# A row maximum split in two, statistics behind routing work, and dispatch sends one step sooner, in a vision-text attention and mixture-of-experts kernel

## What is computed

```python
h = tok_ref(x, ...)                      # patches -> 36 tokens, with a layer norm
h = concatenate([h, txt], axis=1)        # (64, 113, 128)
h = h + attn_ref(layernorm(h), Wq, Wkv, Wo, bo)
h = h + ffn_ref(layernorm(h), gate_w, expert_bias, shared..., expert...)

# attn_ref: 8 heads of 64
scores = einsum('bqhd,bkhd->bhqk', q * scale, k).astype(bfloat16)
probs  = softmax(scores, axis=-1)        # row maximum subtracted first
out    = einsum('bhqk,bkhd->bqhd', probs, v) @ Wo + bo
# ffn_ref: a shared expert, and 3 of 16 experts per token
affinity = sigmoid(xf @ gate_w.T)
_, sel = top_k(affinity + expert_bias, 3)
gating = affinity[sel] / sum(affinity[sel])
out = shared(xf) + sum(gating * expert[sel](xf))
```

## Time and profile before

| | |
|---|---|
| median of 3 runs | 810.36 us (809.16 to 811.22) |
| the profiled execution | 811.83 us, its span 810.0 us |
| busy in the span | PE 631.4 us (78%), DVE 586.3 (72%), ACT 437.6 (54%), POOL 553.6 (68%) |
| sends, L610 | 192 on POOL, 200.2 us busy, 1043 ns each |
| expert rows out, L629 | 186 on POOL, 182.0 us busy, 979 ns each |
| row maximum, L1324 | 64 on DVE, 69.7 us busy, 1089 ns each |
| chain that ended last | DVE 25%, PE 22%, issue 13%, POOL 10%, DMA 8%, ACT 6% |

### The profile page before, as it was taken

One profiled execution on the slowest core, in us unless ns is written; L12 is line 12 of the kernel. 1 busy time (PEld: TensorE's weight loads), 2 busy tenths in 40 slices (PEclk: granted clock), 3 DMA queues, 4 the chain that ended last, 5 costly groups with the idle time before them and its releaser, 6 DMA issues.

```text
span 810.0 us, 20105 instructions
## 1 busy us (share of the span) xinstructions
PE 631.4 (78%) x6122; PEld 532.1 (66%) x6122; DVE 586.3 (72%) x2030; ACT 437.6 (54%) x1044; POOL 553.6 (68%) x696
## 2 busy tenths in 40 slices
PE   6667899999999999999999679663999889872000
PEld 4445778888888888888888557542888677762000
DVE  0687899999999999999999937343566565653244
ACT  2546878888888888888887623211343233220000
POOL 4364122687878878787877877777577777777464
PEclk9977999999999999999999959967999999997555
DMA  9910000011111111011111245535666565881697
GB/s 315 262 34 19 1 3 1 25 34 33 33 34 33 33 34 33 30 33 36 31 34 33 85 123 149 150 118 164 200 200 197 182 194 175 247 270 35 172 337 223
DMA packets 66444, 88.02 MB, mean 109 GB/s; under 512 B 11612, under 2 KB 58848, under 8 KB 66186
## 3 DMA queue, kind: packets, MB, share of 16 engines
q1 hardware_dynamic: 30420, 34.76, 15.4%
q10 hardware_dynamic: 23824, 28.68, 12.1%
q0 software_dynamic: 12096, 23.30, 8.5%
HBM read 57.32 MB, written 30.87 MB: 109 GB/s over the span
## 4 chain that ended last, share of the span: by engine, by line
DVE 25%; PE 22%; issue 13%; POOL 10%; DMA 8%; ACT 6%; SPq 2%; ACTq 1%; DVEq 0%; POOLq 0%
POOL expert_rows L629 6%; DMA x2t<-expert_rows 4%; DMA expert_rows<-yb,dst_i 3%; PE bank L893 3%; DVE mx L1324 3%; PE bank L687 3%; PE bank L783 2%; POOL dispatched L610 2%; DVE s L1329 2%; DVE vr L1368 2%; PE bank L797 2%; PE bank L902 2%; ACT p L1020 2%; DVE st L1341 2%; DVE o L1362 1%
## 5 line engine op out<-in xcount | busy, mean ns | idle before, releaser
L610 POOL DMA_INDIRECT dispatched<-pay,sloti x192 | 200.2, 1043 | 53.5 <-issue 52.5
L629 POOL DMA_INDIRECT expert_rows<-yb,dst_i x186 | 182.0, 979 | 61.3 <-issue 48.9
L1054 ACT ACTIVATE xe<-bank 128x256 f32<-128x256 f32 x93 | 35.7, 384 | 156.6 <-PE bank L882 132.0
L687 PE MATMUL bank<-xt,wqkv 128*128 128x452 f32 x384 | 100.3, 391 | 7.1 <-issue 5.9
L1445 DVE TENSOR_TENSOR hide<-bank,sge 128x256 f32<-128x256 f32 x93 | 39.3, 422 | 69.4 <-ACT sge L1059 35.3
L687 PEld LDWEIGHTS bank<-xt,wqkv 128*128 128x128 f32 x384 | 67.9, 193 | 14.0 <-issue 8.0
L1324 DVE TENSOR_REDUCE mx<-s 113x8 bf16<-113x904 bf16 x64 | 69.7, 1089 | 2.1 <-ACT s L1026 1.7
L836 PE MATMUL bank<-kt,qt 64*113 64x113 f32 x1024 | 67.1, 270 | 5.1 <-DVE h L1339 5.1
L1455 DVE TENSOR_TENSOR yb<-bank,gd 128x256 f32<-128x256 f32 x93 | 38.9, 418 | 43.4 <-DMA expert_rows<-yb,dst_i 39.9
L893 PE MATMUL bank<-xe,kt 128*128 128x256 f32 (+1 forms) x296 | 66.8, 355 | 2.6 <-issue 2.4
L1026 ACT ACTIVATE s<-bank 113x452 bf16<-113x452 f32 x128 | 63.1, 550 | 5.9 <-PE bank L836 5.8
(11 more groups left out here) (209 smaller groups left out, 1743.3 us busy)
## 6 DMA issues: line engine op xcount, KB each, us to landing
kt<-in_w_ffn ACTq DMA_DIRECT2D x74, 192.0 KB
xs_all<-dispatched SPq DMA_DIRECT2D x77, 140.0 KB
x2t<-expert_rows SPq DMA_DIRECT2D x16, 672.0 KB
vr<-in_w_ffn ACTq DMA_DIRECT2D x35, 192.0 KB
out_h<-h ACTq DMA_DIRECT2D x16, 224.0 KB
x2t<-in_x ACTq DMA_DIRECT2D x4, 864.0 KB, 9.8
x2t<-in_x SPq DMA_DIRECT2D x4, 864.0 KB, 11.3
dispatched<-pay,sloti POOLq DMA_INDIRECT x192
```

The lines of the kernel that those rows point to most:

```text
L610: pool.indirect_dma_start(out=xs_dram[:, :], out_offset=bass.IndirectOffsetOnAxis(ap=sloti[:, q % (PAYS // GRP), b, c:c + 1], axis=0), in_ ...
L629: pool.indirect_dma_start(out=y_dram[:, :], out_offset=bass.IndirectOffsetOnAxis(ap=dst_i[:, slot, j:j + 1], axis=0), in_=yb[t % RW][:, j, ...
L687: m = nc.tensor.matmul(dst, wqkv[:, a, at:at + 128], xg[:, b, :], start=(j == 0), stop=(j == 2))
```

## The change

The row maximum becomes two operations: an elementwise maximum of the first 57 and the last 57 of the 113 scores of each row (the middle one is in both), in bf16 into a new tile `mh`, and a reduction over 57. The first one stands ahead of the second norm (L1319), the second one behind it. The routing operation of point 1 moves from behind L1346 to ahead of L1341. `SENDS` begins one step sooner, and in a step that places a group all sends of the step are issued at its end: 3 sends in each of the steps 10 to 57, 4 in each of 58 to 64, 8 in step 65.

```diff
-SENDS = [3 * max(0, min(n - 10, 48)) + 4 * max(0, min(n - 58, 6)) for n in range(B + 1)] + [B * TOPK - 12]
+SENDS = [3 * max(0, min(n - 9, 48)) + 4 * max(0, min(n - 57, 7)) for n in range(B + 1)] + [B * TOPK - 12]
...
+        mh = sb("mh", [128, H, TP // 2], BF16)
...
-                cuts = [begin, min(begin + 1, end), min(begin + 2, end), end]
+                cuts = [begin, begin, begin, end] if n in PLACED else [begin, min(begin + 1, end), min(begin + 2, end), end]
...
+                if ok(n):
+
+                    after(dve, "s_copied", n)
+                    nc.vector.tensor_tensor(mh[0:T, :, :], s16[i][0:T, :, 0:TP // 2], s16[i][0:T, :, T - TP // 2:T],
+                                            ALU.max).then_inc(S["half_max"], 1)
                 if ok(n - 3):
                     after(dve, "rs2_done", n - 3)
...
-                    after(dve, "s_copied", n)
-                    nc.vector.reduce_max(mx[i][0:T, :], s16[i][0:T, :, 0:T], AX.X).then_inc(S["max_done"], 1)
+                    after(dve, "half_max", n)
+                    nc.vector.reduce_max(mx[i][0:T, :], mh[0:T, :, :], AX.X).then_inc(S["max_done"], 1)
...
                     nc.vector.tensor_tensor(row(n - 2), bank[3][0:T, 0:D], row(n - 2), ALU.add).then_inc(S["h_done"], 1)
+                routing(o, k, 1)
+                if ok(n - 2):
+
                     after_all(dve, ("txt_in", 32), ("h_done", n - 2, 1))
                     nc.vector.bn_stats(st2[0:T, i, :], row(n - 2)).then_inc(S["st2_raw"], 1)
...
                                             ALU.subtract).then_inc(S["xl_copied"], 1)
-                routing(o, k, 1)
                 if ok(n - 2):
```

More of the change, by code:

```diff
@@ L257, in build @@
             "st1_raw st1_done mean1_done ve1_done rs1_done xn_ready xt_done xt_copied qa_done qb_done q_copied k_copied "
-            "v_done v1_done vr_done v_ready "
+            "v_done v1_done vr_done v_ready half_max "
             "s_done s_copied max_done mx2_done sub_done exp_done pt_done pt_copied av_done rec_done o_ready ot_done ot_copied "
```

## The result

The changed kernel took 800.72 us (796.57 to 802.19, 4 runs) against 810.79 us (809.16 to 812.5, 4 runs) for the kernel before: a ratio of 0.9863, 95% interval [0.9826, 0.9901]. All ratios here are those on record, from the fast runs alone, and need not equal the quotient of the two medians. The forecast was 797.0, range 792 to 804. So it is faster, by about 10 us rather than 13. The profiled execution lasted 800.95 us (span 799.1, granted clock 0.901) against 811.83 (span 810.0).

What follows compares the result with a forecast made beforehand. VectorE and TensorE were taken to bound the steps together, GpSimd from about step 59. Rounds 8.2 us plus sends 5.1 us gave 13.3 off the profiled 811.83, 798.5; as a median 797.0, range 792 to 804.

Steps and rivals of the forecast that it cites:

- rival 1: VectorE's elementwise maximum runs at full price because of odd-length rows; a round gains 0.40 us, 800 us in all; chance 0.12.
- The term for 4q+8: Moving the routing operation in step 4q+8 shortens L1339 to L1352 from 1.22 to 1.04 us, a gain of 0.18.
- Rival 2: The moved routing operation covers none of VectorE's wait; a round gains 0.20 us, 803 us in all; chance 0.09.
- Loop B: Path over VectorE, two TensorE steps and one VectorE-bound step: 24.63 us a round, falling to 24.06 as the new bound.
- TensorE's own floor is 4 x 5.68 + 0.28 = 23.0: Least time TensorE needs for a round of four steps, 23.0 us, below the forecast round of 24.06.
- 13 x 0.63 = 8.2: Steps 7 to 58 are 13 rounds, each gaining 0.63 us: 8.2 us in all.
- 8 instead of 12: 4 x 1.28 = 5.1 us: GpSimd in step 65 has four fewer sends at 1.28 us each, so all after it comes 5.1 us sooner.
- rival 3: Tiles don't start sooner because TensorE or the loads hold them; only 8.2 us gained, 802 us; chance 0.09.
- now wait for L1238 ... 0.1 to 0.2 us late costs nothing: In placing steps GpSimd's sends wait for L1238; 0.1 to 0.2 us late costs nothing while GpSimd waits about 1 us.
- The lighter steps before gain nothing that I count: The steps before step 7 were counted with no gain.
- Rival 4: GpSimd's sends hold VectorE's elementwise maximum to 1.0 us rather than 0.31; 13 us slower, 823 us; chance 0.06.
- Rival 5: Nothing moves: the round stays at 24.7 us and the sends' gain goes into later waits, 810 us; chance 0.04.

Runs made afterwards that it cites:

- Experiment 6: Changed kernel with `mh` in fp32, so the elementwise maximum is not all bf16, on the slow chip: 916.53 us, ratio 0.997 to the kernel before.
- experiment 1: Kernel before with only the new `SENDS` and `cuts`: 805.97 us beside 811.75 for the kernel before, ratio 0.9903.
- experiment 2: Changed kernel with `SENDS` and `cuts` of before, both VectorE edits kept: 804.13 us, ratio 0.9896 to the kernel before.
- experiment 3: Changed kernel with the routing operation back in its old place, split maximum and early sends kept: 805.55 us, ratio 0.9913 to the kernel before.
- experiment 4: Changed kernel with the row maximum in one operation again, moved operation and early sends kept: 799.25 us, ratio 0.9846 to the kernel before.
- experiment 12: Changed kernel with early statistics spread over steps 1 to 4 and the maximum directly ahead of the reduction: 793.79 us, ratio 0.9807 to the kernel before.
- experiment 5: Changed kernel again, unaltered, as a control on the next, slow chip: 914.1 us beside 918.09 for the kernel before, ratio 0.9992.
- experiment 8: Changed kernel with one of a placing step's three early sends put off to the next step, slow chip: 909.57 us, ratio 0.9907 to the kernel before.
- experiment 7: Changed kernel with the first-norm statistics of two early groups spread over steps 1 to 4, slow chip: 908.17 us, ratio 0.9897 to the kernel before.
- experiment 9: Changed kernel with the early statistics spread over steps 1 to 4, on a third chip: 793.96 us beside 809.56 for the kernel before, ratio 0.9798.
- experiment 10: Changed kernel with early statistics spread over steps 1 to 4 and the one-operation row maximum: 797.08 us, ratio 0.9847 to the kernel before.
- experiment 11: Changed kernel with early statistics spread over steps 1 to 4 and one early send per placing step put off: 795.73 us, ratio 0.983 to the kernel before.

## Why the prediction was right, and where it was not

**The split.** The maximum was to last 0.39 us with a successor at 0.31, the reduction 0.62: measured 0.401, 0.31 and 0.621. Experiment 6 shows that rival 1's condition (full price) did not hold and what it would cost. The wait without its cover costs 0.12 where I said 0.17. The gain of 0.145 us a step of VectorE's time is there (0.31 and 0.54 for 1.00); that all of it would shorten the round was the wrong part, see below.

**The move.** `h` to the aggregate was forecast at 0.86 (4q+7) and 1.04 (4q+8) and measured at 0.77 and 0.85, so the gains were 0.34 and 0.37 rather than 0.25 and 0.18. In 4q+7, L1345 to L1350 takes 0.39 with L1179 between them; in the step at 276.68 it takes 0.38 with nothing between them: the moved operation is free. The term for 4q+8 was mis-sized: "0.19 (L1339) + 0.46 + 0.39" charged the moved operation with 0.46, and in its new place it takes 0.27 (270.60 to 270.87). The means of its group, 499 ns where it stood and 346 ns where it stands, say that this is no single case. In its old place it started 0.49 us behind the start of a send of GpSimd (298.35 and 297.86), in the new one it starts 0.07 us ahead of one. It has two operands in SBUF, so I take the send for the cause. In its old place it took 0.53 us or more in 11 of 16 cases, and in all 11 it ended within 0.03 us of a send's end, as if that had released it. But the other five ran at 0.34 to 0.36 us, and three of them also started during a send or a row out (322.99 behind a send at 322.15, 444.99 and 490.52); in the changed kernel all 16 ran at 0.34 to 0.36, three of them so placed. So that is argued, not shown.

Rival 2 falls by experiments 1 to 4: moving this one operation takes 0.53 us off a round without the split, and 0.44 with it. The sentence that rival 2 quotes from the Trainium skill (VectorE: DVE Perf Modes, section The DRAIN you can't avoid) does not carry over to these instructions. The trace disagrees: 0.38 us from `h` to its statistics against 0.28 of duration, and 0.43 against 0.31 in experiment 12.

**The round.** I forecast 24.06 from Loop B. It came to 23.75, and Loop B was not the bound. The step that failed is "TensorE's own floor is 4 x 5.68 + 0.28 = 23.0". I had taken the floor from one step and added the ranks. In the changed kernel TensorE is busy 23.41 us in a round and idle 0.34 before L688, by "issue" and not by a wait for any engine: 23.75 together, 0.75 above my floor. The number alone does not show this, since Loop B with the gains that were measured would be 24.63 - 0.34 - 0.37 - 0.145 = 23.78. What shows it is that TensorE's wait for `o`, through which Loop B runs, is gone, and that the split is worth 0.08 a round behind the move where Loop B has it at 0.145. The earlier trace rows had TensorE at 23.68 of 24.68 us. With the 0.42 us of issue in the same timeline that reads as a floor of 24.1, which is 0.35 too high: as the rounds get shorter, TensorE's busy time shrinks too, from 23.65 to 23.39 in the mean of 12 rounds, for the same matmuls. So that sum would not have given 23.75 either, but it would have shown how near the floor was.

A second part is the base: I took one round of 24.69, while the rounds of before average 24.47. The base was 0.22 too high and the forecast round 0.31 too high, so that the gain, 0.63 forecast and 0.72 measured, came out nearly right. That 13 x 0.63 = 8.2 met the measured 8.7 is in part luck. Of the 0.72, 0.11 to 0.16 comes with the sends, which I had put at nothing; by what path I can't show.

**The sends at the end.** "8 instead of 12: 4 x 1.28 = 5.1 us" measured 5.2, and experiments 1 and 2 (11.8 and 16.9 us) show that it is the sends alone. "5.1 us reach the end" held: from the first to the last row out it is 256.8 us after 257.5. So rival 3 is out, on a chip without the idle stretches of experiment 5.

**The sends in steps 58 and 64.** Here a step of the prediction failed: the placing step's sends "now wait for L1238 ... 0.1 to 0.2 us late costs nothing". The wait costs more than the operation it waits for: from the end of L1239 to the start of the send it is 0.86 us (284.85 to 285.71), and 0.86 or 0.87 in all seven waits, where a send that waits for nothing starts 0.19 after L580. Yet the plain operation L579 starts 0.17 us after the end of L1360, for which it waits (283.69 to 283.86). So it is the indirect DMA, and not a wait for VectorE as such, that starts so late. In the rounds GpSimd has the time for it, as I said. In step 58 GpSimd idles 1.03 us for the slots and then has one send more to do, where I had "1.28 us into the idle 1.21"; in step 64 it idles 1.06 us, and I had not looked at that step. From step 58 to `ve` of step 65 GpSimd is busy 0.9 us more (35.89 after 35.00) and idle 0.5 us more: 1.4 us together, as in experiment 1.

**The early steps.** "The lighter steps before gain nothing that I count" left out that they can lose. The 2.9 us are the granted clock, and they are no part of the edit: experiment 1, with VectorE's code of before, and experiments 3, 5 and 8 have step 2 to 5 at 24.4 to 24.5 us with a clock below 1.00 around 90 us and again around 105; experiment 2 has the first fall alone and 22.7; experiments 4 and 6, like the kernel before, have none and 21.5 to 21.7. What they share is TensorE's idle time while VectorE does `first_stats`. Without it (experiments 7 and 9 to 12) the clock stayed at 1.00 in all five. What decides whether it falls in the other kernels is open: experiment 4 has TensorE as idle in 85 to 90 us as the changed kernel (3.19 and 3.15 us busy) and kept 1.00, and so did the kernel before with 3.28 in 100 to 105. Had the clock stayed, the profiled execution would have taken 800.95 - 2.9 = 798.1 us, beside the 798.5 forecast for it. The 1.2 us of chance at the start helped it, so that this agreement is better than the account behind it.

**Rival 4** (slower, the maximum held by GpSimd's sends): 401 ns in the median and 585 in the longest of 64, never near the 0.75 us from which it would decide. Its rule (the Trainium skill, SBUF — State Buffer, section Who interferes with whom) fits L1193, with 0.15 us in the mean, better than the maximum. **Rival 5** is out by the result itself. On the chip of experiments 5 to 8, where the whole kernel was 13% slower, the time is what rival 5 says (0.9992); whether the round stayed there is not known, since the kernel before has no trace on it.

## What to carry to other kernels

When two engines are both nearly always busy in a loop, take the second one's floor from its busy time over the whole loop, idle issue time included, and not from one of its steps: it says about how much of the gain on the first can be had at all (here 24.1 by that reading, 23.0 by one step, 23.75 in the end). A wait between two dependent operations of one engine is room for an independent one, and it is worth more than a faster operation, but only where that engine's chain ends in someone's wait. And when work is sent earlier, look where its inputs become ready in the last rounds as well, where no slack is left.

## What the runs showed of the hardware that I had not expected

The granted clock fell to a mean of 0.66 to 0.67 over two 5 us stretches in the first steps, right behind stretches in which TensorE was busy 3.15 and 3.29 of 5 us. Six projections then took 2.61 us where they took 1.47 before, as these two timelines of TensorE show (the first of the changed kernel, the second of before):

```profile
92.19 2.61 PE L688 MATMUL bank<-xt,wqkv 128*128 128x452 f32 x6
```

```profile
92.98 1.47 PE L687 MATMUL bank<-xt,wqkv 128*128 128x452 f32 x6
```

Two such falls cost 2.9 us, over a quarter of what the change brings, and they come and go between kernels whose code in that stretch is the same. The other surprise is the chip of experiments 5 to 8: the same work on VectorE, ScalarE and GpSimd with the same durations, 13% more time, and a change with a ratio of 0.9863 elsewhere at 0.9992 [0.9943, 1.004] there. Other waits, above all GpSimd's for tile results (84.2 us rather than 9.3), had grown; why, is open.
